# One 4 MB load and one square per row tile, in place of two halves, in a graph-attention kernel

## What is computed

```python
# x: (8192, 128) float32; adj: (8192, 8192) int32, 0 or 1, about 2 ones in a row
h = x @ W                                        # (8192, 128)
e = (h @ a1)[:, None] + (h @ a2)[None, :]
e = where(e > 0, e, 0.2 * e)
e = where(adj > 0, e, -9e15)
attention = softmax(e, axis=1)
x = layernorm(x + elu(attention @ h))
```

## Time and profile before

| what | value |
|---|---|
| median of 3 runs | 725.54 us (724.77 to 726.19) |
| the profiled execution, its time | 724.11 us |
| the profiled execution, span from first to last instruction | 722.3 us |
| busy share of the span: TensorE, VectorE, ScalarE, GpSimd | 78%, 67%, 72%, 61% |
| bytes over the DMA engines | 285.57 MB, mean 395 GB/s |
| mean granted TensorE clock | 0.88 of 2.4 GHz |

### The profile page before, as it was taken

How to read it: one execution, slowest core, us unless ns; L and a number is a source line. 1 busy time by engine, 2 the same in 40 slices (tenths; PEclk the granted TensorE clock), 3 DMA queues, 4 the chain that set the end, 5 groups by cost and what they waited for, 6 DMA issues and landing times.

```text
span 722.3 us, 11927 instructions
## 1 busy us (share of the span) xinstructions
PE 565.0 (78%) x3075; PEld 352.7 (49%) x3075; DVE 484.7 (67%) x2051; ACT 521.0 (72%) x414; POOL 443.4 (61%) x668
## 2 busy tenths in 40 slices
PE   0868799987777888778877877888887887877783
PEld 0323455554445555555544555555445555554472
DVE  1375677776776666676776666677667666676855
ACT  0847678877787877778787878788787877778310
POOL 2016267767666676667676667576767667767641
PEclk9988798999999999988999999688879999999867
DMA  8999999999999999999999999999999999999600
GB/s 353 327 422 422 402 425 427 428 424 423 427 428 427 427 426 427 428 426 428 426 427 427 425 428 428 427 426 428 426 426 429 425 429 428 427 425 415 200 24 23
DMA packets 34438, 285.57 MB, mean 395 GB/s; under 512 B 5496, under 2 KB 13840, under 8 KB 18032
## 3 DMA queue, kind: packets, MB, share of 16 engines
q1 hardware_dynamic: 28864, 276.83, 91.7%
q0 software_dynamic: 5120, 8.42, 3.2%
q10 hardware_dynamic: 432, 0.07, 0.1%
HBM read 283.18 MB, written 4.19 MB: 398 GB/s over the span
## 4 chain that ended last, share of the span: by engine, by line
DMA 62%; PE 13%; ACT 10%; DVE 6%; issue 5%; POOL 1%; SPq 0%; ACTq 0%; POOLq 0%; DVEq 0%
DMA adj_sb<-in_adj 60%; ACT adj_squared L541 10%; PE fold L641 8%; DMA a_sb<-in_L_gnn_a 2%; PE misc L666 2%; PE fold L639 1%; POOL edge_row L359 1%; PE x_att_ps L689 1%; PE small L656 1%; DVE s_all L825 1%; DVE x_times_wa L823 1%; DVE below_end L885 1%; DVE top_map L839 0%; DVE spread L371 0%; DVE row_edge L889 0%
## 5 line engine op out<-in xcount | busy, mean ns | idle before, releaser
L541 ACT ACTIVATE adj_squared<-adj_sb 128x4096 bf16<-128x4096 int32 x128 | 462.7, 3615 | 99.3 <-DMA adj_sb<-in_adj 95.7
L641 PE MATMUL fold<-adj_sb,bit_ident 128*128 128x512 bf16 x1024 | 305.8, 449 | 0.0
L489 POOL DMA_INDIRECT nb<-in_x,index x160 | 165.7, 1035 | 89.6 <-issue 63.9
L641 PEld LDWEIGHTS fold<-adj_sb,bit_ident 128*128 128x128 bf16 x1024 | 110.4, 108 | 154.0 <-issue 67.1
L839 DVE MAX8 top_map<-fold 128x8 f32<-128x512 f32 x128 | 89.5, 700 | 74.6 <-PE fold L641 71.1
L639 PE MATMUL fold<-col_no,ident_bf 128*128 128x512 bf16 x128 | 54.1, 423 | 103.6 <-DMA adj_sb<-in_adj 95.4
L359 POOL TENSOR_SCALAR edge_row<-row_iota,edge_in 128x128 f32<-128x128 int32 x186 | 129.4, 709 | 0.1
L375 POOL TENSOR_TENSOR spread<-edge_row,edge_w 128x384 f32<-128x384 f32 x60 | 51.9, 884 | 74.7 <-DVE edge_w L952 74.7
L469 POOL TENSOR_SCALAR empty_diag<-ident,counts 128x128 f32<-128x128 f32 x64 | 42.2, 665 | 64.0 <-DVE counts L876 35.5
L639 PEld LDWEIGHTS fold<-col_no,ident_bf 128*128 128x128 bf16 x128 | 17.0, 133 | 118.3 <-issue 91.9
L689 PEld LDWEIGHTS x_att_ps<-spread,nb 128*128 128x128 f32 x372 | 57.8, 222 | 10.0 <-issue 4.4
(11 more groups left out here) (120 smaller groups left out, 628.5 us busy)
## 6 DMA issues: line engine op xcount, KB each, us to landing
adj_sb<-in_adj SPq DMA_DIRECT2D x128, 2048.0 KB, 14.7
out<-x_sb SPq DMA_DIRECT2D x2, 1536.0 KB
nb<-in_x,index POOLq DMA_INDIRECT x160
out<-x_sb SPq DMA_DIRECT2D x5, 128.0 KB
out<-x_sb SPq DMA_DIRECT2D x1, 384.0 KB
W_sb<-in_L_gnn_W ACTq DMA_DIRECT2D x1, 64.0 KB, 7.8
x_sb<-in_x SPq DMA_DIRECT2D x4, 0.5 KB, 17.6
a_sb<-in_L_gnn_a ACTq DMA_DIRECT2D x2, 0.5 KB, 15.3
```

Of the source, the lines that this page charges most:

```text
L489: nc.gpsimd.indirect_dma_start(out=nb_of(j, g)[:, c, :], out_offset=None, in_=x[:, :], in_offset=bass.IndirectOffsetOnAxis(ap=index[:, g, ...
L541: nc.scalar.activation(adj_squared[:, h % 2, :], adj_sb[:, h % LOAD_SLOTS, :], ACT.Square, accum_out=half_sum[:, h:h + 1]).then_inc(square ...
L641: last = nc.tensor.matmul(fold[:, h % LOAD_SLOTS, :], bit_ident[:, b, :], adj_low[:, h % LOAD_SLOTS, b * FOLD:(b + 1) * FOLD, 0], start=Fa ...
```

## The change

Each row tile is now one load: 128 partitions x 32 KB, 4 MB, into two neighbouring slots of `adj_sb` (slots 0 and 1 for the first tile of a group, 2 and 3 for the second). SyncE waits, before it issues the load of tile t, until both halves of tile t - 2 have been squared and folded. ScalarE squares a whole tile with one instruction. Its `step` ran three squares, `copy_sums`, `exp_weights` and the fourth square; now it runs the square of the first tile, `copy_sums`, `exp_weights` and the square of the second. TensorE still folds four halves in a group in the same order, but halves 0 and 1 wait for one landing, and so do 2 and 3. The sum of ones is kept per tile, and one reduction at the end of the program falls away.

```diff
-        loaded = [sem(f"loaded{s}") for s in range(LOAD_SLOTS)]
+        loaded = [sem(f"loaded{s}") for s in range(PAIR)]
...
-        landings = lambda i, h: i * (16 * HALVES // LOAD_SLOTS) + 16 * (h // LOAD_SLOTS + 1)
+        landings = lambda i, t: i * (16 * BODY // PAIR) + 16 * (t // PAIR + 1)
...
-                    for h in range(g * 2 * PAIR, (g + 1) * 2 * PAIR):
-                        if not (first(i) and h < LOAD_SLOTS):
-                            sp.wait_ge(squared, i * HALVES + (h + 1 - LOAD_SLOTS))
-                            sp.wait_ge(folded, i * HALVES + (h + 1 - LOAD_SLOTS))
-                        tile = adj_tiles[bass.ds(i * BODY + h // 2, 1), :, (h % 2) * HALF:(h % 2 + 1) * HALF]
-                        nc.sync.dma_start(adj_sb[:, h % LOAD_SLOTS, :], tile.rearrange("o p c -> (o p) c")
-                                          ).then_inc(loaded[h % LOAD_SLOTS], 16)
+                    for t in range(g * PAIR, (g + 1) * PAIR):
+                        if not first(i) or t >= PAIR:
+                            sp.wait_ge(squared, i * HALVES + 2 * (t + 1 - PAIR))
+                            sp.wait_ge(folded, i * HALVES + 2 * (t + 1 - PAIR))
+                        slots = adj_sb[:, 2 * (t % PAIR):2 * (t % PAIR) + 2, :].rearrange("p s c -> p (s c)")
+                        nc.sync.dma_start(slots, adj_tiles[bass.ds(i * BODY + t, 1), :, :].rearrange("o p c -> (o p) c")
+                                          ).then_inc(loaded[t % PAIR], 16)
...
-                def square_half(i, g, q):
-                    h = g * 2 * PAIR + q
-                    act.wait_ge(loaded[h % LOAD_SLOTS], landings(i, h))
-                    if not (first(i) and h < 2):
-                        act.wait_ge(squared, i * HALVES + (h - 1))
-                    if q == 0 and not first(i):
+                def square_tile(i, g, t):
+                    n = g * PAIR + t
+                    act.wait_ge(loaded[t], landings(i, n))
+                    if not (first(i) and n < 1):
+                        act.wait_ge(squared, i * HALVES + 2 * n)
+                    if t == 0 and not first(i):
                         act.wait_ge(sums_kept, count(i, g) - GROUPS)
-                    nc.scalar.activation(adj_squared[:, h % 2, :], adj_sb[:, h % LOAD_SLOTS, :], ACT.Square,
-                                         accum_out=half_sum[:, h:h + 1]).then_inc(squared, 1)
+                    nc.scalar.activation(adj_squared[:], adj_sb[:, 2 * t:2 * t + 2, :], ACT.Square,
+                                         accum_out=tile_sum[:, n:n + 1]).then_inc(squared, 2)
...
-                    square_half(*now, 0)
-                    square_half(*now, 1)
-                    square_half(*now, 2)
+                    square_tile(*now, 0)
                     if p3:
                         copy_sums(*p3)
                     if p2:
                         exp_weights(*p2)
-                    square_half(*now, 3)
+                    square_tile(*now, 1)
...
-                    pe.wait_ge(loaded[h % LOAD_SLOTS], landings(i, h))
+                    pe.wait_ge(loaded[h // 2 % PAIR], landings(i, h // 2))
...
-                    v.after(nc.vector.reduce_sum(expected[:], halves, AX.X))
```

More of the change, by code:

```diff
@@ L140, in graph_attention @@
         minus_one = sb("minus_one", [P, PAIR], fp32)
-        half_sum = sb("half_sum", [P, HALVES], fp32)
-        half_sum_all = sb("half_sum_all", [P, 2 * TILES], fp32)
+        tile_sum = sb("tile_sum", [P, BODY], fp32)
+        tile_sum_all = sb("tile_sum_all", [P, TILES], fp32)
         counts_all = sb("counts_all", [P, 2, TILES], fp32)
@@ L158, in graph_attention @@
         below_end = sb("below_end", [P, PAIR, EDGES], fp32)
-        expected = sb("expected", [P, TILES], fp32)
         short = sb("short", [P, TILES], fp32)
@@ L475, in tally @@
                     tiles = bass.ds(j * BODY + g * PAIR, PAIR)
-                    halves = bass.ds(j * HALVES + g * 2 * PAIR, 2 * PAIR)
                     hold(pool, squared, j * HALVES + (g + 1) * 2 * PAIR, pool_spare)
-                    nc.gpsimd.tensor_copy(half_sum_all[:, halves], half_sum[:, g * 2 * PAIR:(g + 1) * 2 * PAIR]
+                    nc.gpsimd.tensor_copy(tile_sum_all[:, tiles], tile_sum[:, g * PAIR:(g + 1) * PAIR]
                                           ).then_inc(sums_kept, 1)
@@ L987, in count_bad @@
                 def count_bad():
-                    halves = half_sum_all[:].rearrange("p (t h) -> p t h", h=2)
                     tiles = "p (j t) -> p j t"
@@ L997, in count_bad @@
                     v.after(last)
-                    v.after(nc.vector.tensor_tensor(short[:], found_all, expected[:], ALU.not_equal))
+                    v.after(nc.vector.tensor_tensor(short[:], found_all, tile_sum_all[:], ALU.not_equal))
                     v.after(nc.vector.tensor_tensor(bad[:], short[:], over[:], ALU.max))
```

## The result

The changed kernel takes 779.1 us (median of 4 runs, 775.4 to 784.2), the one before 725.4 beside it. The ratio is 1.0755, 95% interval 1.0725 to 1.0784. The forecast was 762 in a range of 740 to 792: right in sign and range, 17 us short in size.

A forecast was written before the change was run, and what follows sets the result against it. DMA loads were taken to bound the kernel. Profiled 724.1 + 29 x 1.09 for groups 4 to 32 + 3.0 at the start + 2.0 at the end = 760.7; with runs' median 1.4 above, 762 us, range 740 to 792.

The forecast's parts named there:

- The loads set the pace: In the steady groups of 20.36 us, the 16 DMA engines never pause, at share 1.01 and 427 GB/s.
- the slack of a slot: Time a slot's load has to spare before it is due: falls from 7.0 to 0.5 us with two buffers.
- The square of 8192 columns: ScalarE's whole-tile square takes 7.0 us; the next load is issued 7.3 us after the square began.
- 12.6 us from the first landing to the second square: Folds, count_starts, sum_neighbours, fill_edges to exp_weights sum to 12.6 us, so the second tile, landing at 10.2, waits.
- The slow first fold: TensorE's first fold after idle time, partly at 1.2 GHz: taken as 3.4 us, the second as 2.0.
- rival 3: Cold folds: TensorE's clock stays at 1.2 GHz through both folds and sum_neighbours, 804 us; chance 0.12, shared with unseen waits.
- 12.6 us for a load that meets empty engines: Issue to landing of a 4 MB load with nothing ahead: 7.7 us for a half plus 4.9 for another.
- the round: Two-group sum from the first tile's landing: 12.6 + 7.3 + 12.6 + 10.4 = 42.9 us, 21.45 per group, 1.09 more.
- The wait for the scores as the cause of the loss: Second tile's square stands behind exp_weights, its chain lacking 1.9 us; this delays the loads, 1.09 us per group.
- The ends: Outside the steady groups: 3.0 us at the start, between 0 and 6, and 2.0 at the end for a second fold.
- Rival 1: Hidden after all: a tile load needs at most 10.8 us, so the queue never runs dry, 728 us; chance 0.10.
- Rival 2: Faster: 32 KB runs halve the packets, saving 5.7 us where the queue stays full, 722 us; chance 0.04.

The follow-up runs named there:

- the third slot: Changed kernel with a third 4 MB tile slot, uint8 squares, loop unrolled to six groups: 748.7 us; with its loop written out, 738.5 us.
- run 2: Changed kernel with one line moved, exp_weights behind the square of the second tile instead of ahead of it: 776.9 us, ratio 1.0723.
- the sweep: Kernel without the computation: 4 MB loads into two slots, each reloaded after a square of 1024 to 8192 columns; 9.71 to 10.62 us per tile.

## Why the forecast had the sign and missed the size

- **"The loads set the pace", and the change spends the slack of a slot:** right, and the heart of it. Shown by the third slot. That 0.5 us of it would be left was wrong: in run 2, with no wait for the scores, a slot needs 0.2 + 7.3 + 14.5 = 22.0 us, 1.7 more than the 20.3 of before.
- **The square of 8192 columns, 7.0 us, issue 7.3 us behind it:** right, 7.03 and 7.3.
- **12.6 us from the first landing to the second square:** right, 12.4 in the mean. The slow first fold was part of it (3.5 us in the mean), and rival 3 did not come: the second fold took 2.4 in the mean and over 3 in 2 of 26 groups.
- **12.6 us for a load that meets empty engines:** 12.1 measured. The Trainium skill, "DMA: Bandwidth & Descriptors", section "Anatomy of one DMA", gives 2.0 us plus bytes / 436 GB/s, as a fit for DMAs issued from GpSimd, an estimate of 11.6 and 6.8 us for the two sizes; here 12.1 and 7.2, that is some 2.4 us plus bytes / 432 GB/s. For 4 MB the page and I were each 0.5 us off, to either side. Both answered the wrong question.
- **The step that failed is the round:** "12.6 to the issue's landing; then A's load, which was in the queue, 10.4". It treats a queue as either empty or full. Measured in the changed kernel, the two terms are 13.4 and 11.0, and 12.4 + 7.3 + 13.4 + 11.0 = 44.1 for two groups, not 42.9. In the mean a load is issued 2.4 us (second tile) or 3.4 us (first) before the one ahead lands, and in that state time is lost: the engines stand empty for a part of it, and the packets are slower. In the sweep, loads issued 3.5 us ahead in the mean cost 0.9 us more than those issued 4.3 us or more ahead. The term that was too small is the 12.6 us from issue to landing: with another load under way it was 14.5 for a slot that did not wait. With that, the first tile's slot, to which I gave 0.5 us to spare, is as late as the second's. Neither a load by itself nor a load in a full queue shows this, and the trace of before held no other kind in its steady part.
- **The wait for the scores as the cause of the loss:** wrong, though the wait itself was there (133 us in the run). Taken away in run 2, it changed the time by 2 us, within the intervals; the load grew by nearly what the wait had been, 1.1 us.
- **Luck:** without the wait, the forecast's own sum leaves 0.5 us to spare and no loss in the steady part. Its sign and most of its size hung on a wait that turned out to be free, and the true cost, 14.5 in place of 12.6 us, happened to be of the same order. That 779 lies in the range is in part luck.
- **The ends:** 2.0 at the end was 2.7, 3.0 at the start was 6.7. I had no row for the second, and took the middle of my bounds, 0 to 6, where it was above the top. Of the 19.6 us that the span is over the forecast (778.5 against 722.3 + 36.6), 16 lie in the 28 groups behind the 8th tile (1.67 each in place of 1.09), the rest at the ends.
- **Rival 1** (hidden) needed loads issued 4.3 us ahead, and these were 2.4 to 3.4 ahead in the mean. **Rival 2** (longer rows faster): they are 0.7% faster in a full queue, 4.5 us for the whole of adj at most; in the kernel with three slots no such gain shows.

What stays open: why a change of loads with little overlap costs time. The trace shows where. In the changed kernel, packets that begin in the first us of a load take 1.64 us in the mean, and those of its third to tenth us 1.22 to 1.25. With three slots, those of the first us take 1.32. Whether that is the fetch of descriptors, the order of the 16 engines or the memory, no run here tells. The stalls of the loop of six groups are located at its jump; that they are a fetch of code is argued from the one packet in each, not tested by itself. Why the loop written out costs 11 us stays open too. And no version here beats the kernel before: in this kernel the 2 MB loads in four slots already hold the DMA engines at full rate.

## What to carry to other kernels

- Two buffers of twice the size are not the same as four: what counts is how long before the landing ahead of it a load is issued. For two buffers, work it out as (time of one load in a full queue) less (time from landing to release). With 4 MB loads here, a result of 4.3 us lost nothing, 3.4 lost 5% of the rate and 2.5 lost 9%. Four slots of 2 MB had 7 us in hand.
- The longest wait in the table need not be the loss. Follow each slot's round, landing, release, issue, landing: its sum is the pace, and a wait that another piece of the round makes good is free. A forecast's signs can nearly all come true without telling its story from another, so name beforehand the one that would.
- Before an instruction is moved, ask what it releases. The second fold looked like 2 us of TensorE; as the last reader of a slot it was worth 90.

## What the runs showed of the hardware that I had not expected

- Loads of 4 MB issued 3.5 us in the mean before the one ahead of them lands take 14.0 us to their landing, more than the 12.1 of a load by itself, and the rate falls to 391 GB/s at a DMA share of 0.96.
- Five gathers of 64 KB for two tiles add 1.1 us, where their bytes at 427 GB/s would be 0.77.
- The same program with its loop written out is some 11 us slower (736.6 against 725.1 beside it), and in a loop of six groups VectorE stalled some 6 us at each of the three jumps back.
